# An xDeepFM forward pass: embedding gathers issued in groups, and the dump of the next tile's rows moved ahead of the reads of xn

## The reference

```python
emb = tables[feat_idx, sparse]                      # (2048, 26, 32)
linear_out = lin_sparse_w[feat_idx, sparse].sum(-1) + dense @ lin_dense_w
x0 = xk = emb
for w, bb in ((conv1_w, conv1_b), (conv2_w, conv2_b)):
    hp = einsum('bhd,bmd->bhmd', xk, x0).reshape(-1, h * M, E)
    xn = sigmoid(einsum('oi,bid->bod', w, hp) + bb[None, :, None])
    xk = xn[:, :half]; res.append(xn[:, half:])     # 128 rows, half go on
cin_out = (concatenate(res, 1).sum(-1) @ cin_w + cin_b)[:, 0]
deep_x = concatenate([emb.reshape(-1, M * E), dense], -1)
h3 = tanh(tanh(tanh(deep_x @ W1 + b1) @ W2 + b2) @ W3 + b3)
return linear_out + cin_out + (h3 @ deep_w + deep_b)[:, 0] + bias[0]
```

## Time and profile before

| | |
|---|---|
| median of 3 runs | 1602.87 us (1598.68 to 1613.62) |
| the profiled execution, its own time | 1607.53 us |
| its span, first to last instruction | 1605.7 us |
| mean granted clock of PE | 0.993 |
| busy: PE, DVE, POOL, ACT | 94%, 71%, 43%, 40% of the span |
| transfers | 322.08 MB, 200 GB/s over the span |
| tiles, by the first K fill of tile 0 and of tile 15 | 61.77 to 1252.87 us |

### The profile page before, as it was taken

How to read it: one execution, slowest core, us unless ns; L and a number is a source line. 1 busy time by engine, 2 the same in 40 slices (tenths; PEclk the granted TensorE clock), 3 DMA queues, 4 the chain that set the end, 5 groups by cost and what they waited for, 6 DMA issues and landing times.

```text
span 1605.7 us, 23632 instructions
## 1 busy us (share of the span) xinstructions
PE 1515.2 (94%) x6552; PEld 662.5 (41%) x6552; DVE 1133.7 (71%) x1113; ACT 646.7 (40%) x904; POOL 682.6 (43%) x600
## 2 busy tenths in 40 slices
PE   0598999999999999999999999999999999999999
PEld 0233333333333333333333333333333337787876
DVE  3385878788888887878787877788876785343442
ACT  2333443444444344334444443434443433444443
POOL 7356564546464646454555546464631010000000
PEclk9998999999999999999999999999999999999999
DMA  6686989888998899988898989898999993846741
GB/s 130 132 228 170 230 217 222 197 232 204 241 216 233 201 232 198 233 200 232 206 241 208 236 198 236 203 247 200 246 194 240 234 243 105 187 129 167 166 134 53
DMA packets 177869, 322.08 MB, mean 201 GB/s; under 512 B 30160, under 2 KB 106032, under 8 KB 177796
## 3 DMA queue, kind: packets, MB, share of 16 engines
q1 hardware_dynamic: 128250, 287.98, 70.8%
q10 hardware_dynamic: 36273, 26.61, 6.9%
q0 software_dynamic: 13312, 7.06, 4.4%
HBM read 300.24 MB, written 21.31 MB: 200 GB/s over the span
## 4 chain that ended last, share of the span: by engine, by line
PE 75%; DMA 9%; issue 4%; DVE 3%; SPq 2%; ACTq 2%; POOL 2%; ACT 1%; another core or an unknown queue 0%; DVEq 0%; POOLq 0%
PE acc L800 37%; PE acc L794 16%; PE bc L937 14%; DMA x0t<-x_halves 6%; PE bc L780 4%; PE bc L787 3%; ACTq L388 2%; POOL emb L572 2%; DMA emb<-table,idx_stage 2%; SPq L490 1%; DVE xb L747 1%; DVE hp L747 1%; DMA x_halves<-deep_halves 1%; PE bc L772 1%; DMA xb<-x_rows 1%
## 5 line engine op out<-in xcount | busy, mean ns | idle before, releaser
L572 POOL DMA_INDIRECT emb<-table,idx_stage x416 | 494.8, 1189 | 335.9 <-DVE hp L747 169.9
L747 DVE TENSOR_TENSOR hp<-bc,xk 128x1024 f32<-128x1024 f32 x384 | 446.3, 1217 | 257.1 <-PE bc L780 172.7
L747 DVE TENSOR_TENSOR xb<-xb,xk 128x1024 f32<-128x1024 f32 x448 | 552.4, 1288 | 15.1 <-DMA xb<-x_rows 14.9
L800 PE MATMUL acc<-xb,w2s 128*64 128x512 f32 x1792 | 408.6, 594 | 0.2
L800 PE MATMUL acc<-hp,w2s 128*64 128x512 f32 x1536 | 362.9, 608 | 6.0 <-ACT r L986 6.0
L794 PE MATMUL acc<-sq,w1s 128*128 128x512 f32 x768 | 349.9, 605 | 2.2 <-issue 2.2
L979 ACT ACTIVATE sq<-bc 128x1024 f32<-128x1024 f32 x192 | 182.9, 1027 | 190.2 <-PE bc L787 144.0
L800 PEld LDWEIGHTS acc<-xb,w2s 128*64 128x64 f32 x1792 | 127.1, 137 | 253.3 <-issue 227.0
L583 POOL TENSOR_TENSOR r<-r 128x512 f32<-128x512 f32 x96 | 128.8, 1342 | 220.6 <-ACT r L990 130.3
L794 PEld LDWEIGHTS acc<-sq,w1s 128*128 128x128 f32 x768 | 141.9, 191 | 181.3 <-issue 181.3
L984 ACT ACTIVATE xk<-acc,bias 64x512 f32<-64x512 f32 x128 | 87.3, 682 | 275.9 <-PE acc L794 164.1
(11 more groups left out here) (61 smaller groups left out, 814.0 us busy)
## 6 DMA issues: line engine op xcount, KB each, us to landing
xb<-x_rows SPq DMA_DIRECT2D x448, 256.0 KB
xb<-x_rows SPq DMA_DIRECT2D x192, 512.0 KB
w_raw<-W SPq DMA_DIRECT2D x48, 512.0 KB
xb<-x_rows SPq DMA_DIRECT2D x128, 128.0 KB
x0t<-x_halves ACTq DMA_DIRECT2D x252, 52.0 KB
x_full<-x_halves SPq DMA_DIRECT2D x96, 128.0 KB
x_halves<-deep_halves ACTq DMA_DIRECT2D x30, 384.0 KB
emb<-table,idx_stage POOLq DMA_INDIRECT x416
```

Source lines behind the costliest of these rows:

```text
L572: nc.gpsimd.indirect_dma_start(out=emb[:, m, :], out_offset=None, in_=table, in_offset=bass.IndirectOffsetOnAxis(ap=idx_stage[:, m:m + 1], ...
L747: nc.vector.tensor_tensor(product(n)[:, :], x[:, :], xk[sl % 2][:, :], ALU.mult).then_inc(multiplied, 1)
L800: last = nc.tensor.matmul(acc_y[H * c:H * c + H, :], w2s[:, ORDER[n], :], src[:, c * CHUNK:(c + 1) * CHUNK], start=(n == 0), stop=(n == PA ...
```

## The change

The lists of work get a third one, `FIRST_TILE_WORK`, for step 1 of tile 0. The deep step is now step 1 in every tile; in tile 0 the D fills stand between the two halves of the squares, DVE makes the low halves ahead of product 5, and SP, not ACT, issues the halves dump, behind the first spread of step 2. In tiles 1 to 14 ACT issues the halves dump right behind its read of y2, ahead of both halves of xn; before, it stood between the two halves. In step 2 the loads of the next tile's `x0t` now stand ahead of the read of y2; before, behind it (in tile 0 between the two halves of xn). And `gather_in` waits once for a group of fields, for the first product of its list, where it waited for one product for each field; the 26 gathers of a tile are grouped 4, 4, 4, 5, 5 and 4. In tile 0, eight gathers go first as before, six wait for one early event each, and the last twelve go behind product 0; the next tile's go 5, 6 and 11.

```diff
--- before.py
+++ after.py
@@ -93,6 +93,20 @@
     ("terms", None),
     ("of_this", (2, 3, 4)),
 )
+FIRST_TILE_WORK = (
+    ("fill", (("K", 0), ("K", 1), ("K", 2))),
+    ("of_last", (5, 6, 7)),
+    ("of_last", (8, 9, 10, 11, 12)),
+    ("fill", (0, 1, 2)),
+    ("first", 0),
+    ("fill", (("D", 0), ("D", 1), ("D", 2))),
+    ("first", 1),
+    ("of_this", (0, 1)),
+    ("fill", (5, 6, 7)),
+    ("of_this", (2, 3, 4)),
+)
+DEEP_STEP = 1
 LEFT = tuple(n for kind, what in STEP_WORK if kind == "of_last" for n in what)
 DEEP_PARTS = range(0, 3), range(3, KD - 1), range(KD - 1, KD)
 SLOTS = 3
...
-def deep_step(ahead):
-    return 2 if ahead == 3 else 1
+def step_work(sl, ahead):
+    if ahead == 0 and sl == STEPS - 1:
+        return FINAL_WORK
+    return FIRST_TILE_WORK if ahead == 3 and sl == DEEP_STEP else STEP_WORK
 def step_fills(sl, ahead):
-    fills = [use for kind, what in STEP_WORK if kind == "fill" for use in what]
-    if ahead == 0 and sl == STEPS - 1:
-        fills = [use for use in fills if not is_k(use)]
-    if ahead == 0 or sl != deep_step(ahead):
-        fills = [use for use in fills if not is_d(use)]
-    return fills
+    fills = [use for kind, what in step_work(sl, ahead) if kind == "fill" for use in what]
+    return fills if ahead > 0 and sl == DEEP_STEP else [use for use in fills if not is_d(use)]
@@ -388,6 +400,14 @@
                 eng.dma_start(x0t[sl][start:start + 2 * M:2, :].bitcast(F32),
                               rows[:, first:first + Q, :].rearrange("m d b -> m (d b)")).then_inc(x0_loaded[sl % 2], 16)
+        def dump_halves(eng, t):
+            for i in range(2):
+                eng.dma_start(x0_halves[bass.ds(t, 1), i, 0:(KD - 1) * P, :].rearrange("t (k p) b -> p (t k) b", p=P),
+                              deep_halves[:, i, 0:KD - 1, :].bitcast(F32)).then_inc(halves_dumped, 16)
+            eng.dma_start(x0_halves[bass.ds(t, 1), :, (KD - 1) * P:M * ROW, :].rearrange("t i p b -> p (t i) b"),
+                          deep_halves[0:LAST_E, :, KD - 1, :].bitcast(F32)).then_inc(halves_dumped, 16)
         W1_STEPS = 6
         @block.sync
@@ -508,7 +528,11 @@
                             sp.wait_ge(contracted, contracted_by(s - 1, ns[-1]))
                             hold()
                         spread_by_dma(t, sl, i)
-                    if sl == deep_step(ahead) and ahead > 0:
+                        if is_first and sl == DEEP_STEP + 1 and i == 0:
+                            sp.wait_ge(deep_lowered, 2 * DEEP_N)
+                            hold()
+                            dump_halves(sp, t + 1)
+                    if sl == DEEP_STEP and ahead > 0:
                         dump(t + 1)
                     if ahead == 1:
@@ -600,10 +624,9 @@
             def gather_in(s, fields, ns):
-                for m, n in zip(fields, ns):
-                    pool.wait_ge(multiplied, multiplied_by(s, n))
-                    hold()
-                    gather((m,), gathered)
+                pool.wait_ge(multiplied, multiplied_by(s, ns[0]))
+                hold()
+                gather(fields, gathered)
@@ -612,40 +635,42 @@
                 if is_first:
                     free_emb(t, DEEP_N)
                     gather(range(8), gathered)
-                    gather_in(s, range(8, 16), range(8))
+                    for m, (signal, count) in enumerate(((k_contracted, 1), (xk_made, 1), (xk_made, 2), (squared, K1 + 1),
+                                                         (squared, K1 + 2), (squared, 2 * K1))):
+                        pool.wait_ge(signal, count)
+                        hold()
+                        gather((8 + m,), gathered)
+                    gather_in(s, range(14, M), (0,))
                     add_up(t, 1, r1, r1_step, xn_read, 2, sum1)
-                    gather_in(s, range(16, 21), range(8, PAIRS))
-                    gather_in(s + 1, range(21, M), range(5))
                     add_up(t, 2, r1, r1_step, xn_read, 2, sum1)
+                    free_emb(t + 1, filled_by(t, DEEP_STEP, ("D", DEEP_N - 1), ahead))
                     add_up(t, 1, r2, r2_step, y2_read, 1, sum2)
-                    free_emb(t + 1, filled_by(t, 2, ("D", DEEP_N - 1), ahead))
-                    gather_in(s + 2, range(5), (1, 2, 3, 4, 6))
+                    gather_in(s + 2, range(5), (1,))
                     add_up(t, 3, r1, r1_step, xn_read, 2, sum1)
-                    gather_in(s + 2, range(5, 11), range(7, PAIRS))
+                    gather_in(s + 2, range(5, 11), (7,))
                     add_up(t, 2, r2, r2_step, y2_read, 1, sum2)
-                    gather_in(s + 3, range(11, 20), range(9))
+                    gather_in(s + 3, range(11, 22), (0,))
                     return
                 if ahead > 0:
-                    gather_in(s - 1, range(20, 23), (8, 10, 12))
+                    gather_in(s - 1, range(22, M), (8,))
                 add_up(t - 1, STEPS - 1, r2, r2_step, y2_read, 1, sum2)
-                if ahead > 0:
-                    gather_in(s, range(23, M), (0, 1, 3))
                 add_up(t, 1, r1, r1_step, xn_read, 2, sum1)
                 if ahead > 1:
                     free_emb(t + 1, filled_by(t, 1, ("D", DEEP_N - 1), ahead))
-                    gather_in(s + 1, range(4), (0, 2, 4, 6))
+                    gather_in(s + 1, range(4), (0,))
                 add_up(t, 2, r1, r1_step, xn_read, 2, sum1)
                 if ahead > 1:
-                    gather_in(s + 1, range(4, 8), (7, 8, 10, 12))
+                    gather_in(s + 1, range(4, 8), (7,))
                 add_up(t, 1, r2, r2_step, y2_read, 1, sum2)
                 if ahead > 1:
-                    gather_in(s + 2, range(8, 11), (0, 2, 4))
+                    gather_in(s + 2, range(8, 12), (0,))
                 add_up(t, 3, r1, r1_step, xn_read, 2, sum1)
                 if ahead > 1:
-                    gather_in(s + 2, range(11, 15), (7, 8, 10, 12))
+                    gather_in(s + 2, range(12, 17), (7,))
                 add_up(t, 2, r2, r2_step, y2_read, 1, sum2)
                 if ahead > 1:
-                    gather_in(s + 3, range(15, 20), (0, 2, 4, 6, 7))
+                    gather_in(s + 3, range(17, 22), (0,))
             over_tiles(pool, tile)
             add_up(TILES - 1, STEPS - 1, r2, r2_step, y2_read, 1, sum2)
@@ -726,7 +751,7 @@
                     s = t * STEPS + sl
                     start = is_first and sl == 0
                     for n in range(PAIRS):
-                        if n == 0 and sl == deep_step(ahead) and ahead > 0:
+                        if n == (5 if is_first else 0) and sl == DEEP_STEP and ahead > 0:
                             dve.wait_ge(gathered, t * GATHERED + GATHERED)
                             sum_linear(t + 1)
                             for i, ks in enumerate(DEEP_PARTS):
@@ -865,7 +890,7 @@
                     start = is_first and sl == 0
                     final = ahead == 0 and sl == STEPS - 1
                     there = step_fills(sl, ahead)
-                    for kind, what in FINAL_WORK if final else STEP_WORK:
+                    for kind, what in step_work(sl, ahead):
                         if kind == "fill":
                             uses = [use for use in what if use in there]
@@ -989,16 +1014,6 @@
                 act.wait_ge(contracted, s * PAIRS + PAIRS)
                 nc.scalar.activation(r2[:, sl, :], acc[sl % 2][:, :], ACT.Sigmoid, bias=bias2[:, :]).then_inc(y2_read, 1)
-            def dump_halves(t):
...
-                    turning = sl == deep_step(ahead) and ahead > 0
-                    late = turning and sl == 2
...
-                    for kind, what in STEP_WORK:
-                        if kind == "of_last" and what[-1] == PAIRS - 1 and ("K", 0) in there and sl != 2:
+                    for kind, what in step_work(sl, ahead):
+                        if kind == "of_last" and what[-1] == PAIRS - 1 and ("K", 0) in there:
                             load_next_rows()
                         if kind == "fill":
                             for use in what:
@@ -1057,17 +1068,12 @@
                                 act.wait_ge(r2_step, t * SUMS - (SUMS - 1))
                             if sl == STEPS - 1 and not is_first:
                                 act.wait_ge(r2_step, t * SUMS - (SUMS - (STEPS - 1)))
-                            if late:
-                                dump_halves(t + 1)
                             read_y2(s - 1, (sl - 1) % STEPS)
-                            if sl == 2 and not late:
-                                load_next_rows()
+                            if sl == DEEP_STEP and ahead > 0 and not is_first:
+                                act.wait_ge(deep_lowered, t * DEEP_N + 2 * DEEP_N)
+                                act.sem_inc(act_held, 1)
+                                dump_halves(act, t + 1)
                         elif kind == "first" and ("K", 0) in there:
```

(12 more changed lines are left out.)

## The result

| | before | after |
|---|---|---|
| median of the runs | 1604.05 us (1598.68 to 1613.62, 4 runs) | 1649.38 us (1640.93 to 1652.05, 4 runs) |
| ratio, 95% interval | | 1.0267 (1.0205 to 1.0329) |
| profiled execution, mean granted clock | 1607.53 us, 0.993 | 1652.05 us, 0.982 |
| tile 0 over its floor of 77.16 us | 10.0 us | 4.2 us |
| tiles 1 to 14 over their floor | 23.7 us | 75.0 us |

Slower by 2.7%, where 1586 was forecast. The last two rows hold nearly all of it: 1652.05 − 4.2 − 75.0 = 1572.8, which is close to the prediction's floor of 1573.8. By the step's place in the tile, the 75.0 us of tiles 1 to 14 are 10.4 in step 0, **64.5 in step 1**, 0.1 in step 2 and none in step 3. Before, most stood in step 2 (19.1 of 23.7).

The account below looks back on a forecast made before the run. PE's own matmuls were taken to bound the kernel, with 33.7 us of waiting within reach. Floor 1573.8 plus 2.6 (tile 0), 5.6 (xn) and 4 (late spreads) gave 1586 us; range 1576 to 1602.

Parts of the forecast that it names:

- floor: PE's matmuls without waiting: 77.16 us a tile; the profiled 1607.53 us less 33.7 of waiting gives 1573.8.
- The dump goes ahead of xn on ACT in tiles 1 to 14: Step 1: PE waits for xn when the third issue exceeds 2.9 us; 0.4 a tile, 5.6 us, bounds 0 and 14.
- 3.4 at worst: Step 1, tiles 1 to 14: the new xn wait per tile if the third issue kept its longest old price, 6.31 us.
- the wait moves onto xn: Rival, step 1: third issue stays at 3.60 us or more, 14 us of new waits, one or two clock falls; 1597, chance 0.20.
- Tile 0: Turning tile 1 in step 1 leaves 2.6 us of the 10.0 us of waiting, at the second contraction of squares; bounds 0 and 10.
- `x0t` waits: PE's waits for the next step's rows, 14.2 us in nine waits before; none were to remain behind tile 0.
- slower: Rival: the dump delays SP's spreads for products 10 to 12, DVE and PE wait; 1631 in all tiles, 1604 in half; chance 0.10.
- Cost nothing: Step 2: loads ahead of the last sum's read land some 4 us earlier at no cost; without that cover, a few us.
- no new wait: Rival, step 1: the third issue costs 1.05 us at its new place, so the 5.6 us go; 1579, chance 0.15.
- late spreads and their like: Tile 14 waits for spreads while SP also loads the dense layers' rows; 4 us left in the sum for that and its like.

Follow-up runs that it names:

- e3: The kernel after with the dump's third transfer issued behind half 1 of xn, the first two left early; 1597.05 us, 0.9916 of the kernel before.
- e5: The kernel after with the 90 KB transfer of the halves dump issued ahead of the two of 384 KB; 1601.08 us, 0.9957 of the kernel before.
- e7: The kernel after with SP's spreads of pairs 8 to 12 in step 1 of tiles 1 to 14 cut to a quarter of their columns; 1588.55 us, 0.9876.
- e4: The kernel after with SP issuing the halves dump in tiles 1 to 14, behind its dump of the rows; 1593.91 us, 0.9869 of the kernel before.
- e1: The kernel after with ACT's halves dump moved back between the two halves of xn in tiles 1 to 14; 1600.72 us, 0.996 of the kernel before.
- e8: The kernel of e4 with the gathers of tiles 1 to 14 waiting one by one again; 1594.55 us, 0.9919 of the kernel before.
- e9: The kernel of e4 with the 90 KB transfer issued first, on SP; 1595.91 us, 0.9927 of the kernel before.

## Why the prediction was wrong

**The step that failed** is "The dump goes ahead of xn on ACT in tiles 1 to 14". It took 0.4 us a tile, 5.6 in all, with 14 as the far bound; the step cost 64.5 us. (Its own "3.4 at worst" makes 48 in 14 tiles; the bound left that out.) Its form was right: PE waits when the third issue exceeds 2.9 us. In tile 5 that gives 4.92 − 2.9 = 2.0, and 2.33 were measured; the issue let go at 511.55, and xn began 0.28 later. Two of its terms were mis-sized.

- *The issue itself.* I let it end when SP's spreads in front had drained, 13.3 to 14.3 us after the step's mark, and counted on a smaller backlog at the earlier place. The drain came about then (14.1, below), but the issue ended 15.6 us after the mark (511.55 − 495.93), only 2.0 us earlier than before (17.6), though it began 3.7 us earlier. So it grew to a median of 5.32 us. Why it outlasts the drain stays open; e3, e5 and e7 show what makes it short.
- *The lower clock behind most waits.* The forecast had no term for it, only one rival had, for one or two waits. Yet a row in hand showed it: tile 2 waits 2.81 us and its contraction then takes 4.14 us against 2.80. It followed 12 of the 14 waits, at 1.4 to 2.6 us each, a third of the loss.

The rival "the wait moves onto xn" was the right mechanism, at 14 us in place of 64.5.

**What was right.** The floor: 1572.8 against 1573.8. Tile 0: 4.2 us over, where 2.6 were forecast and 10.0 stood before; but only 1.4 of them stand at the second half of the squares, as forecast, and 2.1 in step 1, where nothing was (1.27 for gathered rows, 0.83 for DVE). The `x0t` waits went. The "slower" rival by late spreads did not come: DVE's waits for them fell to 0.7 us. That is with a step 1 that is 4 us longer, though; in e3 and e4, where it is not, they are 25.7 and 23.4 against 14.9 before, still far from that rival's 27 to 55 us. "Cost nothing" for the loads ahead of y2 held in the kernel after (0.1 us in step 2), again with that longer step: e1 shows 8.8 us there and e5 6.3. With ACT's standing removed, e4 runs at 0.9869 of the kernel before, near what "no new wait" gave (1579 / 1602.87 = 0.985). Part of that is luck: e4 has 13.8 us over the floor in tiles 1 to 14, where the sum had 4 for late spreads and their like.

**What the traces say of the earlier trace rows.** I took the missing row of ACT's queue as first-come order. For the start of the dump that fits. In tile 5 of the kernel after SP had issued four spreads (512, 256, 256 and 512 KB, 1.57 MB) ahead of the dump (505.33); in the kernel before all nine, 2.62 MB, stood ahead of it (496.86). SP's queue from its first spread to the half microsecond in which the dump's packets set in, after (502.6 to 510.0) and before (490.4 to 502.0):

```profile
q1 hardware_dynamic: 414, 1.50, 74.3%
```

```profile
q1 hardware_dynamic: 747, 2.56, 84.5%
```

So the dump began when nearly all that stood in front had moved, 14.1 us after the mark, within the 13.3 to 14.3 of the prediction. What did not fit is that the third issue ends there: in the kernel after it ended 1.6 us behind the dump's first packet in tile 5, in the kernel before 0.7 us ahead of it. And behind the start the order is not first-come. Half a microsecond of the kernel after, from 512.0 (queue, packets, MB, share):

```profile
q1 hardware_dynamic: 34, 0.11, 87.9%
q10 hardware_dynamic: 34, 0.02, 18.8%
```

The five spreads that SP issued behind the dump move beside it, packet for packet. Equal counts agree with the rule of the Trainium skill (DMA: Bandwidth & Descriptors, section "Queues, rings and completion order") that each DMA engine takes turns between its queues, packet by packet, which I had weighed and set aside. The 4.6 us before the dump's first packet do not agree with my use of it, by which the dump would start at once, and the short issue that I drew from it didn't follow either: the dump's packets are smaller, so equal turns leave it 0.02 of the 0.13 MB, and they begin late.

**Open.** Step 0 of tiles 1 and 8 takes 4.3 and 5.0 us more in the kernel after; e7 has 4.0 and 3.9 in the same places, e3 and e8 nothing. I did not find what ends those waits, and no run here isolates them. They are most of the 10.4 us in step 0, for which the sum had no term.

## What to carry to other kernels

Before a transfer is issued earlier on an engine that also computes, ask what its queue will do with it there: an issue that stands is a wait in the instruction stream, and whatever is behind it, here the read that PE needs next, stands too. The issue's price must be taken at the new place, or bounded by the end that it had at the old one. Give such transfers to an engine with nothing urgent behind them, or order them so that no issue stands, here the small one ahead of the two large ones. And price each new stall of PE with the slower matmuls that may follow it.

## What the runs showed of the hardware

- *Small after large stands, large after small doesn't.* 90 KB behind 2 × 384 KB, in the kernel after: 4.74 to 7.42 us of issue; 384 KB behind 90 or 90 + 384 KB, in e5: 0.42 to 1.44. On SP, where spreads stand in front too (e9), the large ones took up to 4.76.
- *Packets of a queue begin late while another queue is busy.* In the kernel after, the dump's first transfer was issued at 505.33; ACT's queue moved 2 packets between 508.5 and 510.0, and then, in the half microsecond from 510.0 (queue, packets, MB, share):

```profile
q1 hardware_dynamic: 48, 0.14, 69.9%
q10 hardware_dynamic: 109, 0.06, 36.8%
```

That is 4.7 us after the issue. In e7, with SP's spreads cut, it was issued at 487.13 and the queue moved 22 packets in the half microsecond from 488.0 and 197 in the next, about 1.2 us after. The lag is not the length for which the third issue stands: over the 14 tiles the medians are 4.6 us of lag and 5.32 of issue in the kernel after, 5.5 and 3.6 in the kernel before, and in e5 4.5 with no issue over 1.44.

- *The clock did not fall with the length of the wait alone.* A wait of 2.62 us (tile 9) was followed by a contraction of 2.80 us, one of 2.13 (tile 12) by one of 4.22:

```profile
847.43 2.80 PE L825 MATMUL acc<-hp,w2s 128*64 128x512 f32 x12 [2.62 <-ACT r L1011]
...
1090.06 4.22 PE L825 MATMUL acc<-hp,w2s 128*64 128x512 f32 x12 [2.13 <-ACT r L1011]
```

The granted clock of the two stretches was 1.00 and 0.64 (us, busy time of PE, PEld, DVE, ACT and POOL, granted clock, DMA share, GB/s):

```profile
847.40:850.20 2.80, 2.77 (x14) 1.05 (x16) 2.80 (x3) 2.05 (x3) 0.53 (x1) 1.00 1.09 307
1090.06:1094.28 4.22, 4.22 (x14) 1.43 (x16) 4.22 (x5) 2.02 (x3) 1.68 (x2) 0.64 1.10 321
```
